# A four-layer graph network in fp32: a reordered first head, bank release, count loads and last mask

## The reference

```python
def gat(x, W1, a_src1, a_dst1, b1, W2, a_src2, a_dst2, b2, heads, concat):   # layers 0, 1: 4 heads of 512; layer 3: 8 of 96
    h = elu(gat_layer(x, W1, ..., concat=True))
    return gat_layer(h, W2, ..., heads=1, concat=False)                      # 768 wide
def gat_layer(x, W, a_src, a_dst, b, heads, d_out, concat):
    h = (x @ W).reshape(N, heads, d_out)
    e = leaky_relu((h . a_src)[src] + (h . a_dst)[dst], 0.2)
    alpha = softmax of e over the edges that end in one node
    return segment_sum(alpha * h[src], dst) + b
def rgcn_conv(h, src, dst, edge_type, w_rel, w_root, bias):                  # layer 2: three of these, relu between
    xw = einsum('nd,rde->rne', h, w_rel)                                     # 3 relations
    msg = xw[edge_type, src] / count[dst, edge_type]
    return segment_sum(msg, dst) + h @ w_root + bias
```

## Time and profile before

| | us |
|---|---|
| median of 3 runs | 1830.79 (1828.66 to 1831.6) |
| the profiled execution | 1830.77 |
| its span in the profile | 1829.0 |
| PE busy | 1549.6 (85%) |
| DVE, ACT, POOL busy | 865.7, 583.9, 537.8 |
| mean granted clock of PE | 0.918 |

### The profile page before, as it was taken

One profiled execution on the slowest core, in us unless ns is written; L12 is line 12 of the kernel. 1 busy time (PEld: TensorE's weight loads), 2 busy tenths in 40 slices (PEclk: granted clock), 3 DMA queues, 4 the chain that ended last, 5 costly groups with the idle time before them and its releaser, 6 DMA issues.

```text
span 1829.0 us, 27203 instructions
## 1 busy us (share of the span) xinstructions
PE 1549.6 (85%) x10165; PEld 1494.1 (82%) x10165; DVE 865.7 (47%) x2157; ACT 583.9 (32%) x1170; POOL 537.8 (29%) x681
## 2 busy tenths in 40 slices
PE   3977889997878899976899999999999998456787
PEld 3656889897878898976899999999999997456687
DVE  5776776324366763244634223141321224589733
ACT  2323443322334433221332222222221122256521
POOL 3224332332333323322322332323132231322222
PEclk9977999998989999977899999999999999768897
DMA  2221111122211101212111122212123222100012
GB/s 86 75 65 48 47 37 34 35 81 66 85 52 47 42 29 42 79 64 99 56 39 41 53 63 60 58 56 58 33 74 86 71 76 82 44 18 1 2 46 92
DMA packets 88073, 101.63 MB, mean 56 GB/s; under 512 B 9502, under 2 KB 80693, under 8 KB 87946
## 3 DMA queue, kind: packets, MB, share of 16 engines
q1 hardware_dynamic: 71290, 68.86, 13.1%
q10 hardware_dynamic: 16656, 31.07, 5.1%
HBM read 88.12 MB, written 11.78 MB: 55 GB/s over the span
## 4 chain that ended last, share of the span: by engine, by line
PE 60%; DVE 13%; issue 9%; DMA 7%; ACT 6%; POOL 4%; DVEq 1%; ACTq 0%; POOLq 0%; SPq 0%
PE ps L815 36%; PE ps L992 6%; PE ps L878 6%; PE ps L974 4%; DVE prob L1871 3%; DMA xl<-x_scratch 2%; DMA stage<-in_W 2%; PE ps L845 2%; DVE junk L1823 2%; PE ps L1013 1%; POOL pairs L1103 1%; PE ps L950 1%; PE ps L1036 1%; DVE prob L1879 1%; ACT pairs L1192 1%
## 5 line engine op out<-in xcount | busy, mean ns | idle before, releaser
L1103 POOL TENSOR_TENSOR pairs<-stage,pairs 128x256 fp32r<-128x256 f32 (+3 forms) x472 | 371.3, 805 | 862.5 <-ACT pairs L1192 861.6
L815 PE MATMUL ps<-pairs,XB 128*125 128x256 f32 (+2 forms) x2880 | 423.6, 309 | 41.4 <-DVE asp L1823 24.3
L815 PEld LDWEIGHTS ps<-pairs,XB 128*125 128x125 f32 (+1 forms) x2880 | 414.0, 197 | 44.8 <-issue 38.5
L815 PE MATMUL ps<-pairs,XA 128*125 128x256 f32 (+3 forms) x2655 | 379.2, 305 | 11.5 <-DVE asp L1823 6.0
L815 PEld LDWEIGHTS ps<-pairs,XA 128*125 128x125 f32 (+2 forms) x2655 | 374.0, 191 | 13.4 <-DVE asp L1823 6.4
L1192 ACT ACTIVATE pairs<-stage 128x256 fp32r<-128x256 f32 (+3 forms) x472 | 188.9, 423 | 551.6 <-PE ps L815 417.4
L878 PE MATMUL ps<-AT,Hg 125*128 125x314 f32 (+1 forms) x1080 | 165.7, 314 | 7.1 <-ACT full L1250 4.0
L1520 DVE TENSOR_TENSOR Hl<-ps,Hl 125x768 fp32r<-125x768 f32 (+3 forms) x57 | 43.6, 818 | 265.7 <-ACT Hl L1242 265.7
L878 PEld LDWEIGHTS ps<-AT,Hg 125*128 125x128 f32 (+1 forms) x1080 | 160.7, 190 | 8.5 <-ACT full L1250 4.6
L845 PE MATMUL ps<-ident,prob 125*125 125x125 f32 x475 | 87.5, 337 | 78.1 <-ACT full L1250 32.0
L845 PEld LDWEIGHTS ps<-ident,prob 125*125 125x125 f32 x475 | 77.1, 242 | 85.4 <-ACT full L1250 33.2
(11 more groups left out here) (212 smaller groups left out, 1690.1 us busy)
## 6 DMA issues: line engine op xcount, KB each, us to landing
stage<-in_W SPq DMA_DIRECT2D x192, 128.0 KB, 2.3
stage<-in_rel SPq DMA_DIRECT2D x99, 192.0 KB, 2.4
stage<-in_root SPq DMA_DIRECT2D x91, 64.0 KB, 1.8
x_scratch<-xo ACTq DMA_DIRECT2D x15, 375.0 KB
xl<-x_scratch ACTq DMA_DIRECT2D x15, 375.0 KB
stage<-in_rel SPq DMA_DIRECT2D x42, 128.0 KB, 2.1
stage<-in_root SPq DMA_DIRECT2D x12, 192.0 KB, 2.4
stage<-in_W SPq DMA_DIRECT2D x12, 192.0 KB, 2.5
```

Source lines behind the costliest of these rows:

```text
L815: last = mm(o, X[:rows, xi, a, P * (s0 + t):P * (s0 + t) + m], pair(n, b), start=k == 0 and i == 0 and t * pitch % BANK == 0, stop=k == le ...
L1103: nc.gpsimd.tensor_tensor(pair(n, 1), staged(n), pair(n, 0).bitcast(F32), ALU.subtract).then_inc(*up("weights_lo", "weights lo", n))
```

## The change

1. **First head of layers 0 and 1.** `attention_T` 0, 1 and 2 stand behind the second, third and fourth following `scored` tile; they stood behind the whole first half-matrix and its `rows_lo`. `part(first, 4, 6)` stands between the first two. In layer 0 `graph(4)` moves from ahead of `scored(0)` to behind `attention_T` 1, with all its DVE, ACT, POOL and SP pieces.
2. **Banks.** `held` loses each group of banks when ACT's and DVE's reading of it (`rows`) is passed in the list, no longer all at the end of the matrix. The numbers of the banks that follow change through layers 0 and 1.
3. **Layer 1 into layer 2.** `pick_rows` splits off from `embed_operands` and stands ahead of `output` 3; `embed_operands` moves behind `early`; `embed` behind `late`. `count_columns(0, 0)` moves behind `output` 3, 1 to 4 behind `embed`. The five loads of `cr_in`, one to each `output` in ACT's queue, become five in a row in SP's queue.
4. **Last mask.** Its load and its five tiles move into the third relational layer (`AGAIN_AFTER`); only two memsets (`pads_again`) are left at the old place.

```diff
+AGAIN_AFTER = {(0, 1): (0, 1), (0, 2): (2, 3), (1, 0): (4,)}
...
         if h < 0:
+            if l:
+                yield ("part", first, 0, 4)
             yield from (("score_sum", l, n), ("spread", l, n), ("scores", l, n))
             if not l:
                 yield ("part", first, 0, 4)
+            yield from scored(n, 0)
+            yield from scored(n, 1)
+            yield ("split", first, k1[0])
+            yield from scored(n, 2)
+            yield ("attention_T", l, n, 0)
+            yield ("split", first, k1[1])
+            yield ("part", first, 4, 6)
+            yield from scored(n, 3)
+            yield ("attention_T", l, n, 1)
             if not l:
                 yield ("graph", NT - 1)
...
+            yield from scored(n, 4)
+            yield ("attention_T", l, n, 2)
+            yield ("split", first, k1[2])
+            yield ("softmax", l, n, 4)
...
+    if l == 1:
+        yield ("pick_rows",)
     yield ("output", l, 3)
     if l == 1:
-        yield ("embed_operands",)
+        yield ("count_columns", 0, 0)
     yield from normalized(l + 1, 2)
     if l == 1:
         yield ("split", FIRST_MATRIX[2], 0)
-        yield ("embed",)
     yield ("norm_in", l + 1, 3)
     yield ("output", l, 4)
     yield ("norm_T", l + 1, 3)
     yield ("early", FIRST_MATRIX[l + 1])
     if l == 1:
-        yield ("count_columns", 0, 0)
-        yield ("count_columns", 0, 1)
+        yield ("embed_operands",)
     yield from normalized(l + 1, 4)
     yield ("late", FIRST_MATRIX[l + 1])
     if l == 1:
-        for d in range(2, NT):
+        yield ("embed",)
+        for d in range(1, NT):
             yield ("count_columns", 0, d)
...
+                if i == 3:
+                    if (c, r) == (0, 0):
+                        yield ("graph_load",)
+                    for d in AGAIN_AFTER.get((c, r), ()):
+                        yield ("graph_again", d)
...
-                            held.clear()
...
+                elif kind == "rows" and s[1][0] != "combine_rows":
+                    for g, (s0, ns, pitch) in enumerate(groups(s[1][-1])):
+                        first_bank = place[fill_of["rows", s[1], g]]
+                        held.difference_update(range(first_bank, first_bank - (-ns * pitch // BANK)))
...
+                if s[0] == "split_to":
+                    sp.wait_ge(*at("filled", "rows", ("project2", 1, 2, 256), 1))
+                    for w in (NW - 2, NW - 1):
+                        sp.wait_ge(*at("counts out", w))
+                    for d in range(NT):
+                        sp.dma_start(cr_in[:, d, :].rearrange("p (r n) -> p r n", r=R),
...
-                    act.wait_ge(*at("filled", "combine_tile", 1, NT - 1, R - 1))
+                elif kind == "graph_load":
+                    act.wait_ge(*at("filled", "rows", ("relation", 3, 0, 0, 384), 0))
+                    act.wait_ge(*at("stage lo", 2, 1, 2))
```

104 lines of the change are left out of this document (53 added, 51 removed).

## The result

The changed kernel takes 1804.7 us in the median (1802.89 to 1808.17, 4 runs) beside 1829.72 (1826.77 to 1831.6) before: a ratio of 0.9867, 95% interval 0.9846 to 0.9888. It is faster, by 25 us and not by the 42 that were forecast, and the time lies above the range (1779 to 1801).

The account below looks back on a forecast made before the run. PE was taken as the bound, busy 1549.6 of 1829.0 us, so only its waits counted. 4.4 + 0.5 + 6.0 - 0.5 + 14 + 17.7 = 42.1 off 1830.77 gave 1789 us, range 1779 to 1801.

Parts of the forecast that it names:

- The last mask: Way into layer 3: without the mask there PE's 24.35 us wait shrinks, 17.7 us gained; relational layer 0, up to -3.
- Layer 0's first head: Layer 0, first head: block of 60 matmuls and degree transpose start earlier, 4.4 us gained (0 to 6).
- Layer 1's first head: Layer 1, first head: second half's matmuls begin slightly earlier, at a bank `full` frees; 0.5 us gained (-1 to 2.5).
- the -0.5 (-2 to 1) for the heads: Later aggregates: bank waits go, but `spread` waits for DVE and one group for the elu's sum; 0.5 us lost.
- The two waits of the second matrix: Second matrix, layers 0 and 1: waits of 2.99 us each for `dots` go, 6.0 us gained together (3 to 6).
- the waits of about 1.3 us ahead of the aggregates: Later aggregates: these waits were to go too, within the term of -0.5 us.
- rival (5): Dense stretch: throttled clock lengthens its 612.22 us; at 0.936 all gain is eaten, at 0.92 1842 us; chance 0.02.
- rival (3): All waits gain their upper bounds because PE returns from shorter pauses at the higher clock: 1779 us; chance 0.15.
- the 14: Layer 1 into layer 2: reordered passage lets `degrees` start earlier, 14 us gained (8 to 17.5).
- I count nothing, up to 3.6 against: Passage into layer 2: five count loads in SP's queue over output 1's `xl` cost 0, at most 3.6 us.
- rival (1): Passage into layer 2: DVE's counts set the end or loads hold `xl` up; 8 us for 14, 1795; chance 0.16.
- 4 x 2.9: Passage into layer 2: DVE's column counts 1 to 4 at 2.9 us each, from about 869, before `degrees`.

Follow-up runs that it names:

- the steering: Changed kernel with the bank ring steered at four places in the heads and second matrix of layers 0 and 1: 1789.95 us, ratio 0.9798.
- the gate: Changed kernel with count load 0 left in place and the other four issued only once output 3's residual has landed: 1796.06 us.

## Why the prediction was wrong

**The last mask was right**, 17.7 forecast, 17.95 measured, and it cost the relational layer 0.5 us at most (the run with the mask alone). PE's idle time in this stretch fell by 18.2. The run with the mask alone gains 21 there, and the same code takes 162.9 to 168.2 us from one changed kernel to the next, so that the agreement to 0.3 us is partly luck.

**Layer 0's first head was right** in its mechanism: 4.4 forecast, 3.87 against the profiled execution, 2.9 against the changed kernel with the old head. The trace of before happened to be 1.2 us slower in this head than the two other kernels with the same code there. The table switches cost their 1.28 each and no more, with 0.01 us to the next instruction; the page of the Trainium skill that I weighed ("ScalarE: Activation LUTs", section "What ACT_TABLE_LOAD costs", 2.66 us a switch) did not hold in this place.

**Layer 1's first head: the sign was wrong.** 0.5 forecast, -2.2 measured, shown by the run with the old order there (43.30). I had looked at what `full` releases, and not at what the earlier first transpose pushes back: `part(first, 4, 6)`, 30 matmuls, used to run while the first `prob` was made (2.80 us of wait) and now stands behind it (6.36). What the head won at `full` (9.23, now 5.53) it gave back there: PE is idle for 13.27 us in it, and was for 13.35. The 2.2 us are slower matmuls, 32.25 us of busy time for 29.97 at a granted clock of 0.81 for 0.84; with the old order in the changed kernel it is 29.68.

**Banks: the step that failed is the -0.5 (-2 to 1) for the heads.** The two waits of the second matrix went, and brought 6.0 and 4.7, more than the 3.0 each. In layer 0 that was luck: with the rule alone the wait of 2.98 stays, and it goes only where the new order of the first head, or the steering, has moved the ring too. In layer 1 it goes with the rule alone, but it is back with layer 0's head alone reordered. In the heads the prediction reckons with the waits of about 1.3 us ahead of the aggregates; those of 2.08 and 0.95 us behind the third transposes of the two third heads, which the trace of before had already, it doesn't mention. Whether the second half-matrix begins in a bank that DVE has long left or in one that it is just splitting depends on where the ring stands when a head begins, and the change moved that for every head. The heads came out at -5.1. In the second head of layer 0 it is 8.9 us from the third transpose to the block of 60 (228.72), where it was 5.2 in the trace of before, 6.8 in the run with the mask alone and is 5.2 with the ring steered. The prediction also had the rule the wrong way round in words: the banks of a matrix are given back later in the list than before, at `rows` and not with the last matmul. That is why the next group passes them over. The steered ring shows the size, 13 to 15 us, and that it is not the waits: PE's idle time is the same, its matmuls are 20.1 us faster in the profiled executions. That the matmuls keep their time was the silent premise of the whole sum. The clock stood in it as rival (5), for the dense stretch, and as rival (3), with the sign turned round; the heads, where it fell, were not looked at.

**Passage: the 14 was the largest error**, 0.67 measured. Two terms failed. "I count nothing, up to 3.6 against" for the count loads in SP's queue: the residual of output 2 came 17.5 us behind its issue, PE waited 7.68, worked slower behind the pause, and the gate gave 8.9 us back. I had placed the loads at 808 to 826 us and bounded it by the residual of output 1. They were issued from 798.75 on, that residual was for POOL 10.4 us behind its issue, and they met the next one too. And the wait ahead of `degrees`: the mechanism and its place were forecast, rival (1), and 4 x 2.9 was close to the measured 12.8 us from 871 to 884, but the chain began when the rest was already late. Counted from the last spread, DVE was to start on the counts at 71.2 us (869 less 797.77) and started at 82.6, which is 11.4 of the 13.3 us; the chain itself took 2 longer than forecast. Rival (1) was nearer than the forecast, with a price that was too small. In the relational layers 2.5 us more went. PE's idle time there is the same (11.0 and 10.9 us) and its busy time 2.6 longer; these layers take 505.6 to 506.1 us in the three kernels in which `degrees` waits some 2.4 us, and 506.8 to 508.5 in those in which it waits longer.

The misses add up: passage 13.3, relational layers 2.5, layer 1's first head 2.7, layer 0's 0.5, the other heads 4.6 (-5.1 for -0.5), less 4.7 more in the second matrices, 0.3 in the mask and 3.4 by which the two executions differ elsewhere (start, way into layer 1, end). That is 15.2, and 42.1 forecast less 26.9 between the two spans is 15.2.

## What to carry to other kernels

When a change moves the point at which a ring of buffers stands, look at every later user, not only at those that wait now: list for each which buffer it gets and who reads it last, before and after. Compare busy and idle time by stretch: a sum of waits says nothing on what the matmuls between them will take, and here half of the miss lay there. A step that is moved ahead on an in-order engine is paid by what then stands behind it. Loads that nobody needs for some 70 us (issued from 799, used from 871) should be gated behind those that somebody waits for.

## What the runs showed of the hardware

- 2.3 MB of count loads in one row slowed a 375 KB residual, from its issue to POOL's use of it: 17.5 us (811.06 to 828.56), against 9.4 with the gate, 9.7 beside one count load in the kernel before. The mean over 800 to 835 us is 124 GB/s in the changed kernel. The Trainium skill ("Trainium Kernel Development and Optimization", section "Key Constraints") says that the queues of all issuing engines run on the same 16 DMA engines, and that several issuers only save issue time. The runs are in line with it and don't prove it: with the loads back in ACT's queue and spread over the outputs the passage is 5.4 us shorter, with four of them held back in SP's queue 8.9, and no run changes the queue and leaves the times alone.
- DVE's column pick takes 0.79 us with POOL quiet. In the changed kernel the picks that begin while POOL splits weights (871.86, 873.41, 876.88, 879.61) take 1.60 to 1.62, the four others 0.80. That fits what the Trainium skill says ("SBUF — State Buffer", section "SBUF: two separate sides") of a pair of ports that DVE and POOL share as an exclusive lock; I ran nothing that takes POOL away alone.
- 30 matmuls of 256 columns in the second head of layer 0 take 3.77 and 3.79 us behind one pause of PE of 3.22 (before) or 2.33 (steered), with the granted clock at 1.00 throughout. They take 5.04 behind one of 4.64 (the mask alone), 5.31 behind one of 2.17 (the banks alone), where the clock fell to 0.50 only when they were running, and 5.42 behind two of 2.61 and 1.24 (the changed kernel). So the pause just ahead doesn't decide: the shortest single one was followed by slow matmuls, a longer one was not.
